# A three-stage attention and mixture-of-experts kernel: set-up work at two stage take-overs dealt out, two loads moved ahead, record scatters placed elsewhere

## What is computed

```
x = x + tanh(g_xattn) * cross(layernorm(x), ctx)
      cross: q, k, v projections with bias, 16 heads of 32,
             scores / sqrt(32) + relative bias, softmax, values, output projection
x = x + tanh(g_ffn) * ffn(layernorm(x))
      ffn:   h = y + attention(rmsnorm(y))      causal, 16 heads of 64, keys and values from a
                                                latent of 64, rotary part of 32
             h + moe(rmsnorm(h))                shared expert + weighted sum of the best 2 of 8
                                                experts, silu(x Wg) * (x Wu) Wd, inner size 256
```

## Time and profile before

| What | Value |
|---|---|
| median of 3 runs | 2297.93 us (2295.79 to 2301.08) |
| the profiled execution | 2299.8 us, its span 2297.9 us |
| TensorE matmuls busy | 2103.8 us, 92% of the span |
| weight loads (PEld, beside the matmuls) | 957.9 us, 42% |
| VectorE busy | 1493.7 us, 65% |
| GpSimd busy | 1375.5 us, 60% |
| ScalarE busy | 1179.0 us, 51% |
| TensorE's granted clock, mean | 0.969 of full speed |

### The profile page before, as it was taken

The page is one execution under the profiler, slowest core; times in us unless marked ns, Lnnn a source line. Parts: engine busy times, 40 slices in busy tenths (PEclk is TensorE's granted clock), DMA queues, the critical chain, the costliest instruction groups (busy, mean ns, idle before and its releaser), DMA issues.

```text
span 2297.9 us, 43310 instructions
## 1 busy us (share of the span) xinstructions
PE 2103.8 (92%) x12568; PEld 957.9 (42%) x12569; DVE 1493.7 (65%) x4180; ACT 1179.0 (51%) x2319; POOL 1375.5 (60%) x1450
## 2 busy tenths in 40 slices
PE   2899999999999986799999999999997898999998
PEld 1333333333333321344444444444443444455554
DVE  3688888888888885466565665656554778444443
ACT  3355555555555544255455454545545664555554
POOL 3276777677767776157556665655654476555554
PEclk7999999999999997999999999999998899999999
DMA  5513233232323231635445353544551685766665
GB/s 164 168 51 116 72 104 97 88 111 79 111 72 104 80 121 48 180 93 169 130 138 163 105 162 110 162 135 132 150 168 43 145 189 110 125 113 116 112 110 92
DMA packets 227829, 272.09 MB, mean 118 GB/s; under 512 B 40136, under 2 KB 165820, under 8 KB 227364
## 3 DMA queue, kind: packets, MB, share of 16 engines
q1 hardware_dynamic: 197180, 212.69, 30.8%
q0 software_dynamic: 22752, 47.86, 12.2%
q10 hardware_dynamic: 7704, 9.20, 1.2%
HBM read 161.76 MB, written 86.54 MB: 108 GB/s over the span
## 4 chain that ended last, share of the span: by engine, by line
PE 71%; DVE 7%; DMA 6%; POOL 6%; issue 5%; ACT 3%; SPq 1%; ACTq 0%; POOLq 0%; DVEq 0%
PE a_bank L700 13%; PE a_bank L780 5%; PE a_bank L752 5%; PE b_bank L1498 4%; PE a_bank L765 4%; PE b_bank L1499 4%; PE b_bank L1500 4%; PE c_bank L2620 3%; PE c_bank L2621 3%; PE c_bank L2619 3%; PE b_bank L1578 2%; PE b_bank L1610 2%; PE b_bank L1595 2%; PE b_bank L1596 2%; PE b_bank L1580 2%
## 5 line engine op out<-in xcount | busy, mean ns | idle before, releaser
L504 ACT ACTIVATE a_pt<-a_bank 128x512 f32<-128x512 f32 x512 | 305.6, 597 | 371.3 <-DVE a_bank L611 366.7
L1454 DVE CUSTOM_DVE_ANT_0 b_bank<-b_bank,b_tri 128x256 f32<-128x256 f32 (+3 forms) x512 | 253.2, 497 | 298.9 <-PE b_bank L1596 294.4
L622 DVE CUSTOM_DVE_ANT_0 a_bank<-a_bank,a_strip 128x512 f32<-128x512 f32 x512 | 353.2, 691 | 3.6 <-PE a_bank L765 2.7
L1205 POOL TENSOR_TENSOR b_acc<-b_acc,b_pt 128x256 f32<-128x256 f32 (+2 forms) x384 | 280.7, 753 | 81.9 <-ACT b_pt L1318 71.1
L414 POOL TENSOR_TENSOR a_acc<-a_acc,a_pt 128x512 f32<-128x512 f32 x256 | 317.8, 1277 | 16.0 <-ACT a_pt L504 15.6
L611 DVE TENSOR_TENSOR a_bank<-a_bank,a_band 128x256 f32<-128x256 f32 (+1 forms) x512 | 205.7, 402 | 131.5 <-PE a_bank L752 130.3
L1318 ACT ACTIVATE b_pt<-b_bank 128x256 f32<-128x256 f32 (+2 forms) x384 | 144.6, 383 | 182.7 <-PE b_bank L1580 165.9
L752 PE MATMUL a_bank<-a_q_stack,a_k_stack 128*128 128x512 f16 x512 | 199.4, 390 | 23.4 <-ACT a_pt L504 14.0
L765 PE MATMUL a_bank<-a_k_stack,a_q_stack 97*128 97x512 f16 x512 | 196.7, 384 | 4.8 <-DVE a_low L622 4.7
L2038 POOL DMA_INDIRECT out_dram<-c_z,c_to_row x71 | 112.5, 1585 | 132.7 <-DMA out_dram<-c_z,c_to_row 99.8
L1578 PE MATMUL b_bank<-b_q_stack,b_k_stack 96*128 96x256 f16 (+3 forms) x512 | 157.1, 307 | 13.5 <-ACT b_pt L1318 7.9
(11 more groups left out here) (342 smaller groups left out, 5356.6 us busy)
## 6 DMA issues: line engine op xcount, KB each, us to landing
b_q_stack<-qk_rows SPq DMA_DIRECT2D x192, 128.0 KB, 2.7
a_q_stack<-qk_rows SPq DMA_DIRECT2D x96, 128.0 KB
a_k_stack<-qk_rows SPq DMA_DIRECT2D x96, 128.0 KB
b_k_stack<-qk_rows SPq DMA_DIRECT2D x96, 128.0 KB, 2.6
a_sums<-in_x SPq DMA_DIRECT2D x34, 256.0 KB, 3.1
qk_rows<-a_qk_hi SPq DMA_DIRECT2D x64, 128.0 KB, 1.7
qk_rows<-a_qk_lo SPq DMA_DIRECT2D x64, 128.0 KB, 1.8
out_dram<-a_sums SPq DMA_DIRECT2D x32, 256.0 KB, 2.0
```

The costliest lines, as they stand in the source:

```text
L504: nc.scalar.activation(pt[:, n % SLOTS, :], st_bank[n % 2][:], ACT.Exp).then_inc(exped, 1)
L622: nc.vector.tensor_tensor_reduce(out=max_bank[step % 2][:], in0=max_bank[step % 2][:], in1=strip[:, g * HG + hh, at:at + S], scale=-1.0, s ...
L1205: nc.gpsimd.tensor_tensor(sums_of, sums_of, probs(n), ALU.add).then_inc(pooled, 1)
L1454: nc.vector.tensor_tensor_reduce(out=max_bank[step % 2][:, 0:w], in0=max_bank[step % 2][:, 0:w], in1=tri[:, at:at + w], scale=-1.0, scalar ...
```

## The change

- **Causal stage, beginning.** Matrix 0 is split at step 0 and matrix 1 at step 1 as before; the parts of matrix 2 stand at steps 2, 4, 6 and 8, those of matrix 3 at 14, 16, 17 and 20, those of matrix 4 (now in four parts) at 50, 52, 54 and 56. The copies into `far` and `hidden` and the store of the zero row stand at ScalarE's step 7, the seven fills one by one at VectorE's steps 7 to 13; TensorE's waits for them stand at the first HT job and at step 20. Loads are counted on three semaphores in place of two, for matrix 0 to 2 are in flight together.
- **Group 0's rotation** in the first batch stands at step 36 in place of 39.
- **Next rows.** For the kind zero, `xn` is loaded behind `stack` of group 1, as soon as the old rows are turned (the last HT job), ahead of group 1's rotated rows. SP's generator also has one `yield` more, behind the residual load of the kind last.
- **Experts' weights of batch 0** (number 1) are loaded behind a new `yield` ahead of `prior.all_used`, so before the last stores of the causal stage's end.
- **`find_spare`** stands behind the low halves of the next batch's rows (`low` 3), ahead of the low halves of the weights.
- **Scatters.** From batch 2 on one tile stands ahead of the first low part, none between the two, and all others behind the second.

```diff
--- before.py
+++ after.py
@@ -857,7 +857,7 @@
...
-        w_loaded = [sem(f"w_loaded{i}") for i in range(2)]
+        w_loaded = [sem(f"w_loaded{i}") for i in range(3)]
@@ -929,7 +929,10 @@
...
                  "last": [G3], "end": []}
-        turn_step = {G3: 16, "k": 29, 0: 39, 1: 52, 2: 61}
+        turn_steps = {G3: 16, "k": 29, 0: 39, 1: 52, 2: 61}
+
+        def turn_step(kind, r):
+            return 36 if (kind, r) == ("first", 0) else turn_steps[r]
@@ -1012,7 +1015,10 @@
...
                  (wo_hi[:], wo_lo[:], wo.rearrange("(g p) n -> p g n", p=P), P, NG, D)]
-        SPLITS = {0: 0, 1: 1, 2: 2, 3: 9, 4: 50}
+        SPLITS = {0: (0, range(NK)), 1: (1, range(1)), 50: (4, range(0, 1)), 52: (4, range(1, 2)), 54: (4, range(2, 3)), 56: (4, range(3, 4))}
+        SPLITS.update({at: (2, range(k, k + 1)) for k, at in enumerate((2, 4, 6, 8))})
+        SPLITS.update({at: (3, range(k, k + 1)) for k, at in enumerate((14, 16, 17, 20))})
+        SETUP, CONSTANTS = 7, 20
@@ -1023,13 +1029,13 @@
...
             src = staged(n)
-            if n in (0, 2, 3):
-                return [(hi[:, k, :], lo[:, k, :], src[:, k, :], wn[:, 1, k:k + 1]) for k in range(nk)]
+            if n != 1:
+                return [(hi[:, k, :], lo[:, k, :], src[:, k, :], WS if n == 4 else wn[:, 1, k:k + 1]) for k in range(nk)]
...
         for n in range(len(loads)):
-            splits_before.append(splits_before[-1] + (NK if n in (0, 2, 3) else 1))
+            splits_before.append(splits_before[-1] + (1 if n == 1 else NK))
@@ -1077,12 +1083,12 @@
...
                     sp.wait_ge(w_split, splits_before[n])
-                sp.dma_start(staged(n), src).then_inc(w_loaded[n % 2], 16)
+                sp.dma_start(staged(n), src).then_inc(w_loaded[n % 3], 16)
...
                     sp.sem_inc(past_first, 1)
-                if kind in ("first", "zero", "steady"):
+                if kind in ("first", "steady"):
@@ -1103,6 +1109,9 @@
...
                     stack(kind, b, 1)
+                    sp.wait_ge(job_done, upto(kind, b, (HT, NT - 1)))
+                    sp.nop(nofuse=True)
+                    sp.dma_start(xn[:], x1[1:2, :, :].rearrange("a (t p) n -> p (a t) n", p=P)).then_inc(x_loaded, 16)
@@ -1126,6 +1135,7 @@
...
                     residual(b)
+                    yield
@@ -1206,9 +1216,9 @@
...
                     for r in turns[kind]:
...
                             rotate(kind, b, r, False)
@@ -1331,10 +1341,16 @@
...
                                              bias=small[:, u, 2, t:t + 1]).then_inc(z_ready, 1)
-                    if kind == "first" and step in SPLITS.values():
-                        split([n for n in SPLITS if SPLITS[n] == step][0])
+                    if kind == "first" and step in SPLITS:
+                        split(*SPLITS[step])
+                    if kind == "first" and step == SETUP:
+                        act.wait_ge(const_loaded, 64)
+                        nc.scalar.activation(far[:], idn[:], ACT.Copy, scale=1e15).then_inc(far_set, 1)
+                        nc.scalar.activation(hidden[:], later_keys[:], ACT.Copy, scale=1e-15).then_inc(far_set, 1)
+                        act.wait_ge(zero_set, 1)
+                        act.dma_start(zero_row.rearrange("a (c n) -> a c n", n=P), zero[:].unsqueeze(1).broadcast_to([1, NK, P])).then_inc(zeroed, 16)
                     for r in turns[kind]:
@@ -1352,17 +1368,13 @@
...
-            def split(n):
-                act.wait_ge(w_loaded[n % 2], 16 * (n // 2 + 1))
-                for hi, _, src, scale in split_parts(n):
+            def split(n, parts):
+                act.wait_ge(w_loaded[n % 3], 16 * (n // 3 + 1))
+                if n in (0, 2, 3):
+                    act.wait_ge(norm_scaled, 1)
+                for hi, _, src, scale in [split_parts(n)[i] for i in parts]:
...
-            act.wait_ge(zero_set, 1)
-            act.dma_start(zero_row.rearrange("a (c n) -> a c n", n=P), zero[:].unsqueeze(1).broadcast_to([1, NK, P])).then_inc(zeroed, 16)
-            act.wait_ge(norm_scaled, 1)
-            act.wait_ge(const_loaded, 64)
-            nc.scalar.activation(far[:], idn[:], ACT.Copy, scale=1e15).then_inc(far_set, 1)
-            nc.scalar.activation(hidden[:], later_keys[:], ACT.Copy, scale=1e-15).then_inc(far_set, 1)
@@ -1431,9 +1443,10 @@
...
-            def split(n):
+            def split(n, parts):
                 done = splits_before[n]
-                for i, (hi, lo, src, scale) in enumerate(split_parts(n)):
+                for i in parts:
+                    hi, lo, src, scale = split_parts(n)[i]
@@ -1457,23 +1470,24 @@
...
                         moments(b, step - MOMENTS)
-                    if kind == "first" and step in SPLITS.values():
-                        split([n for n in SPLITS if SPLITS[n] == step][0])
+                    if kind == "first" and step in SPLITS:
+                        split(*SPLITS[step])
+                    if kind == "first" and SETUP <= step < SETUP + len(fills):
+                        nc.vector.memset(*fills[step - SETUP]).then_inc(padded, 1)
+                    if kind == "first" and step == CONSTANTS:
+                        dve.wait_ge(const_loaded, 64)
...
                     for r in turns[kind]:
...
-            for a, fill in ((ones_f, 1.0), (rc, 0.0), (rs, 0.0)):
-                nc.vector.memset(a[:], fill).then_inc(padded, 1)
-            for rows in (wb_hi[R:P, :], wb_lo[R:P, :], lat_hi[R + DH:P, :], lat_lo[R + DH:P, :]):
-                nc.vector.memset(rows, 0.0).then_inc(padded, 1)
+            fills = ((ones_f[:], 1.0), (rc[:], 0.0), (rs[:], 0.0), (wb_hi[R:P, :], 0.0), (wb_lo[R:P, :], 0.0),
+                     (lat_hi[R + DH:P, :], 0.0), (lat_lo[R + DH:P, :], 0.0))
...
             dve.wait_ge(norm_scaled, 1)
-            dve.wait_ge(const_loaded, 64)
@@ -1562,6 +1576,11 @@
...
                         pe.wait_ge(first_pass.left_dve, first_pass.upto((O, NT - 1)))
+                    if kind == "first" and step == pieces[HT, 0][0]:
+                        pe.wait_ge(const_loaded, 64)
+                    if kind == "first" and step == CONSTANTS:
+                        pe.wait_ge(far_set, 2)
+                        pe.wait_ge(padded, 7)
@@ -1613,9 +1632,6 @@
...
-            pe.wait_ge(const_loaded, 64)
-            pe.wait_ge(far_set, 2)
-            pe.wait_ge(padded, 7)
@@ -1892,14 +1908,18 @@
...
             yield
+            up_weights(1)
+            down_weights(1)
+            yield
...
             for b in range(B):
-                up_weights(b + 1)
-                down_weights(b + 1)
+                if b:
+                    up_weights(b + 1)
+                    down_weights(b + 1)
@@ -2001,17 +2021,15 @@
...
                 if b > 1:
-                    scatter_some(b, 2)
+                    scatter_some(b, 1)
                 low_part(b, 0)
-                if b > 1:
-                    scatter_some(b, 1)
...
                 if b:
-                    scatter_some(b, 2 if b > 1 else NT)
+                    scatter_some(b, NT)
@@ -2424,8 +2442,6 @@
...
                     settle(b)
-                    if b == 0:
-                        find_spare()
@@ -2437,6 +2453,8 @@
...
                     low_part(0)
+                if b == 0:
+                    find_spare()
...
```

8 lines of the change are left out of this document (4 added, 4 removed).

## The result

The changed kernel takes 2313.26 us (median of four, 2310.41 to 2317.03) against 2296.86 (2295.11 to 2301.08) of the kernel before: ratio 1.0061 [1.0042, 1.0079], some 14 us slower (the two medians alone lie 16.4 us apart). The profiled execution took 2317.03 us with a span of 2314.7; that is 17.2 more than before where I had summed -9.1.

A forecast was written before the change was run, and what follows sets the result against it. TensorE was taken as the bound, busy nine tenths almost everywhere, so only dips pay. Terms -0.5 - 5.3 - 7.5 + 1.8 + 2.4 = -9.1 took the profiled 2299.8 to 2290.7, or 2289 as median; range 2279 to 2298.

The forecast's parts named there:

- Part 4: Experts' scatters: batch 2 gains 6.6 us, late weights cost more, sum +1.8 (bounds -6.6 and +6); plus +2.4 at the end.
- late weights of 3.4, 1.8 and 3.2: Experts' batches 3, 4 and 5: later output addition delays SP's weight loads, adding 3.4, 1.8 and 3.2 us.
- Part 1: Causal beginning dealt out: -3.5 set-up, -2.4 weights 2, +1.2 step 4, +4.2 weights 3; sum -0.5 us, bounds -4.7 and +4.
- The end: After batch 6's second low part: more scatters follow, the last 2.5 us later; +2.4 us, bounds 0 and +4.
- Part 3: Experts' batch 0: earlier weights remove ScalarE's 11.66 us wait, find_spare comes later; -7.5 us, bounds -5 and -10.
- Part 2: Causal next rows: 9.25 us wait goes, group 1's rotated rows come 3.9 later; -5.3 us, bounds -9.2 and -2.
- the term of about -9: Next rows: alternative by the skill's fit, a 4.4 us load giving about -9 us; not the one adopted.
- The set-up: Causal beginning: memsets, `far`, `hidden` and constants' wait leave the queue heads, removing 3.5 of TensorE's 5.37 us wait.
- the four late parts: Causal steps 14, 16, 17 and 20: uncovered parts of weights 3 cost 4.2 us together.
- The slower one: Experts' batches 3 to 5: weight waits lower TensorE's clock; +8 gives 2297 (chance 0.08), past +14 2303, slower (0.07).
- Weights in time: Experts' batches 3 to 5: rings carry earlier loads faster, no late weights; -17.5 us, 2280, chance 0.17.
- Thin covers: Batch 0 gives 3 instead of 7.5 us, next rows 2 instead of 5.3; -1.3, 2297, chance 0.20.

The follow-up runs named there:

- gap8: Changed kernel plus one short GpSimd fill between fourth and fifth of eight scatters: 2300.45 us, 0.9986 on chip 14; repeated on chip 1: 2314.68 us, 1.0060.
- no4: Changed kernel with the scatters placed as in the kernel before: 2292.28 us, ratio 0.9965.
- only4: Kernel before with only the scatters placed as in the change: 2315.85 us, 1.0071; repeated unchanged on chip 1 (only4_again): 2318.89 us, 1.0082.
- only3: Kernel before with only the experts' batch 0 weights loaded sooner and find_spare placed later: 2293.13 us, ratio 0.9973.
- p23: Kernel before with only next rows loaded sooner, batch 0's weights loaded sooner and find_spare later: 2291.64 us, ratio 0.9955.

## Why the prediction was wrong

**Part 4, the failing step.** "The second low part then starts when its high part is there, and the batch is 19.3: -6.6", then late weights of 3.4, 1.8 and 3.2. That costed one queue, GpSimd to SP to the rings. Where signals are on time the waits are those that I had named: in `gap8` on chip 14 ScalarE waits three times for `in_Wu`, 5.7 us together, the longest the 2.12 above. Its batches 2 to 5 are 21.5, 21.5, 23.2 and 19.8, together +1.1 against the 84.8 before, predicted +1.8. That the sum is so near is in part luck: batch 2 gained 4.5 and not 6.6, for it now waits 1.88 us for weights too, behind the late addition of batch 1's row, and batches 3 to 5 paid 2.2, 3.9 and -0.5 where 3.4, 1.8 and 3.2 stood. Even so the whole change with this order was worth 0.9986 there, 3 us and not 9, because of part 1 and the end. What the step left out is that the eight scatters now stand across the moment in which TensorE hands over to ScalarE, where before two tiles of them stood on either side with the addition between. In a session like those on chips 9, 10 and 1 that costs 2 to 6 us a batch and hides the weights. The size of it: `gap8` on chip 1 less `gap8` on chip 14, 1.0060 - 0.9986 = 0.0074, or 17 us; I had nothing for it. The part as a whole, from the changed kernel to `no4`: 1.0061 - 0.9965 = 0.0096, 22 us, or 16 and 19 by `only4` and `only4_again`, where the prediction had 1.8 + 2.4 = 4.2.

**The end.** Predicted +2.4; batch 6 with the end is +6.1 in the profile after and +3.9 in `gap8` on time. The direction was right, the term too small: against the second low part of batch 6 the last scatter comes 4.1 us later in both (21.4 behind it, 17.3 before), not 2.5, for four scatters more take 5.1 and there was only 1 us of pause to fill. VectorE's wait for the first entry, 0.22 us before:

```profile
1965.31 0.15 DVE L2434 CAST c_from_row<-c_entry 128x1 int32<-128x1 f32 x1 [4.19 <-DMA c_entry<-table]
```

**Part 3, right.** -7.5, bounds -5 and -10: batch 0 became 24.5 to 27.4 in every profile that has it (-6.7 to -9.6), and `only3` alone gave 0.9973, 6 us. `find_spare` did move in front of the low halves and the activation, as the step said. VectorE and then ScalarE after:

```profile
1789.48 3.23 DVE L2302 TENSOR_SCALAR c_filler<-c_slot,c_left_out 128x128 f16<-128x128 f32 x16
1792.64 2.73 DVE L2238 SCALAR_TENSOR_TENSOR c_gu_lo<-c_gu_stage,c_wn,c_gu_hi 128x512 f16<-128x512 f32 x4
```

```profile
1780.80 0.60 ACT L2118 ACTIVATE c_th<-c_bank 128x512 f32<-128x512 f32 x1 [8.72 <-DVE b_sums L1424]
...
1796.72 0.63 ACT L2124 ACTIVATE c_h_hi<-c_hid 128x512 f16<-128x512 f32 x1 [3.90 <-DVE c_hid L2391]
```

Counted up I had 16.2 us from tanh to the second high part; it is 15.92. The spread is the clock: in the six profiles with 24.5 us TensorE had its upper level all through the batch, in the seven with 27.1 to 27.4 it had the lower one for 6.8 us, in `only3` (25.9) for 3.4 and before for 13.7; I had allowed 0.9 us for it.

**Part 2, right in kind.** The 9.25 us wait of the earlier trace rows is gone, and SP's queue shows what it was exchanged for, against the earlier trace rows:

```profile
958.11 0.40 SPq L1114 DMA_DIRECT2D b_xn<-out_dram  x1
959.60 0.34 SPq L1044 DMA_DIRECT2D qk_rows<-b_qr_hi  x1
966.95 1.68 SPq L1048 DMA_DIRECT2D b_q_stack<-qk_rows  x3
```

Group 1's rotated rows take 7.35 us instead of 2.51 from store to load (5.2 in `p23`); 3.9 was the term. The stretch, -0.4 here, is 3.1 to 6.6 shorter in seven of the thirteen profiles with this part (5.8 in `p23`) and within 0.6 of before in the other six (without the part it is 84.1 to 89.3). What parts the two groups is how long the 1 MB load took to land: 5.8 to 7.3 us in the seven, 7.8 to 8.6 in the six (7.77 here); why it takes the one or the other is open. The second thing left out is the clock. Here TensorE's idle time fell by 5.1 us, 18.4 to 13.3, much as forecast, but its granted clock over the stretch fell from 0.92 to 0.88, which is 3.4 us. The -5.3 is right for the first group only. The fit of the Trainium skill ("DMA: Bandwidth & Descriptors", section on the anatomy of one DMA) is given there for transfers issued from GpSimd, and this load is issued by SP; its 4.4 us, and the term of about -9 with it, no run shows. With part 3 this is the gain of 0.9955 in `p23`, 10 us; 5.3 + 7.5 = 12.8 were forecast.

**Part 1, the wrong sign.** -0.5 with bounds -4.7 and +4; it is +3.2 to +3.8 in seven of the eight traces with it and +1.4 in `gap8` on chip 14. TensorE's idle times at the take-over after, against the earlier trace rows:

```profile
868.32 0.27 PE L717 MATMUL a_bank<-a_idn,a_low 128*16 128x128 f32 x1 [2.79 <-DVE a_low L622]
871.06 0.61 PE L752 MATMUL a_bank<-a_q_stack,a_k_stack 128*128 128x512 f16 x1 [2.25 <-ACT a_pt L504]
873.92 0.61 PE L752 MATMUL a_bank<-a_q_stack,a_k_stack 128*128 128x512 f16 x1 [2.25 <-ACT a_pt L504]
...
881.96 0.61 PE L752 MATMUL a_bank<-a_q_stack,a_k_stack 128*128 128x512 f16 x1 [2.21 <-ACT a_pt L504]
...
886.80 1.94 PE L709 MATMUL a_bank<-a_acc,a_ones_f 128*32 128x512 f32 x8 [1.48 <-POOL a_acc L414]
...
896.22 0.61 PE L752 MATMUL a_bank<-a_q_stack,a_k_stack 128*128 128x512 f16 x1 [1.79 <-ACT a_pt L504]
899.10 0.61 PE L752 MATMUL a_bank<-a_q_stack,a_k_stack 128*128 128x512 f16 x1 [2.28 <-ACT a_pt L504]
...
907.02 0.61 PE L752 MATMUL a_bank<-a_q_stack,a_k_stack 128*128 128x512 f16 x1 [2.48 <-ACT a_pt L504]
```

5.37, 4.46 and 5.19 have become seven waits of 1.5 to 2.8 (the 1.79 at 896.22 stood there before too). The row-sum matmul (886.80, 886.93) cuts the stretch in two, counted from the 489th exponential:

| us | to the row sums | row sums to step 63 |
|---|---|---|
| before, and six more with its beginning | 26.9 to 27.0 | 23.7 to 25.8 |
| the eight with the beginning dealt out | 24.3 | 29.1 to 31.5 |
| the five with matrices 2 and 3 whole | 25.6, 25.7 | 24.8 to 26.4 |

Ahead of the row sums the gain is 2.7 where -3.5 - 2.4 + 1.2 = -4.7 stood. Dealing out matrix 2 (and taking matrix 3 from step 9) gives 1.4 of it, as costed (1.2), with steps 6 and 8 under the row-sum wait, which shrank from 5.19 to 1.48. The set-up gives 1.3, so "of the 5.37 us I take 3.5 as gone" is the mis-sized term: 2.79 and 2.25 stand in its place, with the split of matrix 0. Behind the row sums the four late parts cost some 6 us, not 4.2. A step with a part takes 2.8 to 2.9 us from one exponential to the next, four times; I had taken 2.2, against 1.02 without:

```profile
895.57 0.60 ACT L504 ACTIVATE a_pt<-a_bank 128x512 f32<-128x512 f32 x1 [0.40 <-DVE a_bank L611]
...
896.58 0.71 ACT L1376 ACTIVATE b_wq_hi<-b_sums,b_wn 128x512 f16<-128x512 f32 x1
898.45 0.60 ACT L504 ACTIVATE a_pt<-a_bank 128x512 f32<-128x512 f32 x1 [1.16 <-DVE a_bank L611]
```

Some 2 of the 6 us may be the clock. The granted clock over this half is 0.69 before and 0.64 here; in seven of the eight traces it is 0.64 to 0.71 and the half takes 30.9 to 31.5 us, in `gap8` on chip 14 it is 0.77 and the half takes 29.1, 4.1 more than before.

**The rivals.** The slower one was priced by the clock behind waits for weights. It was the right side with another cause: the waits were not for weights. (8 to 9 us at half speed are 4.0 to 4.5 us, not the 4.7 that I wrote; and the shares of "faster" add up to 0.63, not 0.70.) The clock did follow. The table by stretch shows the lower level (granted 0.50, 1.2 GHz) right behind TensorE's 3.29 us wait that ends at 1831.30:

```profile
1831.30:1834.70 3.40, 3.40 (x12) 2.28 (x13) 2.56 (x5) 3.40 (x7) 1.14 (x2) 0.50 0.87 98
...
1855.20:1858.60 3.40, 2.91 (x11) 2.15 (x12) 2.56 (x5) 3.40 (x8) 1.66 (x2) 0.50 0.59 81
```

Four such stretches of 3.4 us stand behind four of the five late starts, 1.7 us each at half speed. But from batch 1 to the gather the lower level was granted for 10.5 us before and for 17.1 after, so of the 18 us the clock has some 3.3. The Trainium skill ("TensorE: Matmul & The Clock Gate", section on oscillation) says that waits between bursts put the clock down each time. Here four of five did, each for less time than the 8 us of batch 0 on which I had priced it. Weights in time (2280) was seen only where late signals gave them the time. Thin covers held for part 1 alone.

## What to carry to other kernels

A queue's instructions have two prices: who waits for them, and what they stand beside; when indirect transfers are gathered into one long row, look at which hand-over between other engines falls into it. When a wait is dealt out over steps, each piece costs a handshake of its own (some 1.5 us here, against 0.81 of work), which pays only ahead of a wait that covers it. Where a gain in a dip is counted in idle time, look at the granted clock too: here it took 3.4 us back where the rows came sooner. And run a surprising kernel again beside its rival on one chip: `gap8` was a cure on one chip and nothing on the next.

## What the runs showed of the hardware

- **A row of eight indirect issues on GpSimd can delay what ScalarE hears of TensorE.** ScalarE's copy came 2.7 to 5.9 us after the transposing matmuls instead of 1.2, in 34 of 34 starts with such a row on chips 9, 10 and 1 (and in the first profile), and in 0 of 13 on chips 13, 14 and 7. TensorE's records show the matmuls done at once, and the profile finds no releaser. The semaphore's own updates stand on record as late as the copy (T+5.43 and T+5.49 in the first profile's batch 2), so ScalarE hears the signal at once. Whether TensorE finished when its record says and the signal was held up can't be told from a trace.
- **What makes a chip late is open.** Each chip was used in one session, so chip and session can't be told apart, and which chip gave the first two profiles is not known. Late sessions lack some 1,700 to 2,000 of 35,800 semaphore records, which speaks for something that the signals and the record share, and leaves the recording itself as a rival. The kernel before doesn't show it in its time: 2298.43, 2301.1 and 2302.15 us on the late ones, 2299.4, 2302.8 and 2300.84 on the others, though one of its starts has the row (at batch 2). No spacing of a row of eight other than the short fill (0.12 us) was tried, nor a row of six on a late chip.
- **The same load can land in two times.** The 1 MB of the next rows took 5.8 to 7.3 us in seven profiles and 7.8 to 8.6 in six with the same order around it, and only in the seven was the stretch 3.1 to 6.6 us shorter; why stays open too.
